# Two transformer layers for four sequences on one core: maxima over bank pairs, one top-k for both tiles, early norm statistics, and new orders on all engines

## The chip, the core and the metric

The kernel runs on one core of a Trainium2 chip. Five engines work side by side: PE (matrix multiply; PEld is its weight load), DVE (vector), ACT (scalar functions), POOL (GpSimd) and SP, which here only issues DMAs. Each works through its own list of instructions in order and waits on semaphores. The metric is the device time of one execution in microseconds (us); lower is better.

## The reference, cut to what matters

The input `x` is 4 sequences (batches) of 256 tokens by 256 features. There are two layers of one form, `x = x + attention(norm(x)) * silu(ffn(norm(x)))`.

```python
xn = _layernorm(x)
s = _L0_attn_ref(xn, ...)              # 32 heads of 8, 8 key/value groups, softmax, no mask
g = _silu(_L0_ffn_ref(xn, ...))        # below
x = x + s * g
xn = _layernorm(x)
s = _L1_attn_ref(xn, ...)              # 16 heads of 16, causal, with slopes by distance
g = _silu(_L1_ffn_ref(xn, ...))        # int8 per token, one 256x256 matmul
x = x + s * g

# _L0_ffn_ref: retrieval among 2048 experts
h = silu(xn @ W_up.T + b_up) @ W_down.T + b_down
sim = (h @ W_q.T) . keys               # 2 halves, 8 heads, 45 keys
scores, idx = lax.top_k(sim, 8)        # per half and head
all_scores = sx[:, None] + sy[None, :] # 64 sums per head
all_indices = ix * 45 + iy
sc, pk = lax.top_k(all_scores, 8)      # 8 experts per head, 64 per token
indices = take_along_axis(all_indices, pk)
z = h . down_embed[indices]
out = (silu(z * softmax(sc))) . up_embed[indices]
```

## The kernel before, in words

The 256 tokens of a batch lie as two tiles of 128 partitions. Each batch goes through the same stages, and a stage `name:b.n` is call `n` for batch `b`. The order in which an engine takes the stages is written out by hand in five tables of words (`PE_PLAN`, `ACT_PLAN`, `DVE_PLAN`, `POOL_PLAN`, `SP_PLAN`); in `PE_PLAN` the digits behind the slash are the PSUM banks that the call takes. There are six such banks (`turn`), one 128x512 f32 tile each; a PE call waits until the earlier user of its bank has been drained (`bank`). Batches overlap: work of batch b+1 stands in the lists between that of batch b.

The stages that the change and the prediction speak of:

- Layer 0's norm (`norm0`, DVE `normalise` L1215): statistics, then an inverse root by three Newton rounds of tiny instructions, then the centring (L1232). `norm1` is the same for layer 1.
- The expert side: `up`, `down` and `sim` on PE give the similarities. DVE finds the top 8 per tile: `topv` (L1255) and `topi` (L1261) on the similarities, `topp` (the 64 sums L1267, their best 8), `topl` (L1284 to L1293: the expert numbers by one-hot products of 128x1024 f32), `topw` (softmax weights). `places` splits the numbers in high and low parts; they go by DRAM (`high`) and come back spread over all partitions (`same`, 1024 KB a load), and `match` (L1323) makes one-hots. PE `pick` (L717) takes the dot products, DVE `pick` (L1339, L1341) selects and sums them, `weigh`/`zs` give the factors.
- Then DVE makes `onehot` (L1362) and `scale` (L1373) for each of eight chunks, PE `spread` (L728) multiplies them, and PE `mix` (L738) multiplies with the table of 16 rows per expert part, one call per tile. PE `table` (L704), ACT `firsts`/`seconds` and POOL `left`/`thirds` (L613, L620) split the first table's products in three bf16 parts.
- Attention of layer 0: `qkv0` on PE, `split0` on DVE (three bf16 parts), `store0`/`stack0` on SP (by DRAM into `stackq`, `stackk`). Then `max0`: PE (L816) computes the scores of one head, DVE (L1397) takes each row's maximum out of PSUM, 32 calls a batch. `nm0` splits the maxima and brings them into the stack by a DMA. `sc0` on PE computes the scores again less the maximum, ACT takes the exponential (L1168), `pv0` (L904) multiplies with the values; `ctx0`, `flip0`, `proj0` and DVE `res0` end the layer.
- Layer 1 has `max1` (L836, L1406), `nm1`, `lift1`, `sc1`, `pv1` and so on, run beside layer 0 of the next batch. After the last batch they run alone.

Layer norms and softmax are exact to f32 parts, so most PE work is f32 or three-part bf16.

## Time and profile before

| what | value |
|---|---|
| time, median of 3 runs | 700.35 us (697.94 to 701.03) |
| profiled execution, first to last instruction | 694.5 us |
| what the median has beyond that span | 5.85 us |
| PE busy | 546.2 us (79%) |
| DVE busy | 499.4 us (72%) |
| ACT busy | 264.1 us (38%) |
| POOL busy | 104.5 us (15%) |
| PE's mean granted clock | 0.860 of full speed |

The page gives the profiled execution by its span alone; the runs are timed apart, and no other time of that execution is listed. No engine is busy throughout: PE and DVE take turns at being the late one, so the shares of the whole say little, and the profile is read stage by stage. A stage is cut here by what DVE and PE do: batch 0's top-k ends at 71.7 us, `nm0` of batches 0 to 3 starts at 138.3, 284.9, 458.3 and 606.3, `max0` of batch 1 starts at 219.0, and `ctx0` of batches 1 to 3 at 345.3, 506.5 and 636.8. Busy times are the engine's own; where one instruction's row overlaps the next, their sum is longer than the stretch.

### The profile page before, as it was taken

To read this page: it belongs to the slowest core of one execution; us is meant where nothing else is said; L and a number is where in the kernel's file an instruction comes from. 1 tells how busy PE (TensorE), PEld (TensorE's weight loads), DVE (VectorE), ACT (ScalarE), POOL (GpSimd) and SP (SyncE) were. 2 spreads that over 40 slices of the span, in tenths; PEclk is the share of its full clock that TensorE was granted. 3 is DMA by queue.
4 is the path that set the end of the run, shared out by engine and by line. 5 is a ranking of instruction groups with operands and counts; after the bars stand their busy time and mean duration, and the time that the engine had idled before them with its cause. 6 is when DMAs were issued, how large, how long until landed. Compare 5 with 4: busy or idle time off the path is not lost.

```text
span 694.5 us, 14791 instructions
## 1 busy us (share of the span) xinstructions
PE 546.2 (79%) x5863; PEld 366.2 (53%) x5863; DVE 499.4 (72%) x1469; ACT 264.1 (38%) x550; POOL 104.5 (15%) x75
## 2 busy tenths in 40 slices
...
GB/s 251 106 128 34 139 123 123 1 4 3 122 50 81 123 124 1 4 2 123 1 54 200 78 47 1 1 3 17 51 164 176 123 2 2 0 19 1 1 1 15
DMA packets 15158, 43.40 MB, mean 62 GB/s; under 512 B 3631, under 2 KB 10927, under 8 KB 11986
## 3 DMA queue, kind: packets, MB, share of 16 engines
...
q10 hardware_dynamic: 396, 0.20, 0.1%
q14 instruction: 22, 0.18, 0.1%
...
## 4 chain that ended last, share of the span: by engine, by line
PE 42%; DVE 42%; issue 10%; ACT 4%; DMA 1%; POOL 1%; SPq 0%; ACTq 0%; DVEq 0%
PE experts L738 8%; DVE nmax L1397 6%; PE outs L904 4%; DVE scaled L1373 4%; PE turn L658 4%; PE turn L867 3%; DVE high_hot L1362 3%; PE turn L883 3%; PE turn L704 2%; DVE z L1341 2%; DVE topi L1261 2%; DVE picks L1339 2%; PE turn L836 2%; DVE nwide L1406 2%; PE turn L728 2%
## 5 line engine op out<-in xcount | busy, mean ns | idle before, releaser
L1168 ACT ACTIVATE probs<-turn 128x512 f32<-128x512 f32 x176 | 97.3, 599 | 54.9 <-PE turn L867 21.4
L1397 DVE TENSOR_REDUCE nmax<-turn 128x2 f32<-128x512 f32 x128 | 87.5, 686 | 41.1 <-PE turn L816 40.1
L613 POOL TENSOR_TENSOR left<-left,dots 128x512 f32<-128x512 f32 x32 | 45.8, 1439 | 344.3 <-ACT dots L1051 344.2
L816 PE MATMUL turn<-stackk,stackq 125*128 125x256 bf16 x256 | 57.6, 325 | 35.3 <-DVE nmax L1397 20.0
L738 PE MATMUL experts<-shared,dots 128*128 128x256 f32 x256 | 59.2, 391 | 0.0
L728 PE MATMUL turn<-scaled,high_hot 128*128 128x32 bf16 x1536 | 44.9, 181 | 16.7 <-issue 7.3
L717 PE MATMUL turn<-dots,shared 128*128 128x32 bf16 x1536 | 44.5, 180 | 16.9 <-DVE shared L1323 8.8
L728 PEld LDWEIGHTS turn<-scaled,high_hot 128*128 128x128 bf16 x1536 | 43.6, 100 | 23.7 <-issue 18.4
L717 PEld LDWEIGHTS turn<-dots,shared 128*128 128x128 bf16 x1536 | 43.3, 99 | 24.1 <-DVE shared L1323 13.2
L1061 ACT ACTIVATE dots<-turn 128x512 f32<-128x512 f32 x32 | 18.8, 595 | 94.5 <-PE turn L728 94.3
L738 PEld LDWEIGHTS experts<-shared,dots 128*128 128x128 f32 x256 | 50.4, 199 | 7.4
L867 PE MATMUL turn<-stackq,stackk 128*128 128x512 bf16 x128 | 46.3, 414 | 6.2 <-issue 4.4
L620 POOL TENSOR_TENSOR dots<-left,dots 128x512 bf16<-128x512 f32 x32 | 48.7, 1538 | 13.3 <-ACT dots L1056 13.3
L816 PEld LDWEIGHTS turn<-stackk,stackq 125*128 125x128 bf16 x256 | 20.4, 105 | 56.8 <-DVE nmax L1397 28.0
L904 PE MATMUL outs<-probs,v 128*32 128x256 f32 x512 | 43.2, 411 | 5.6 <-ACT probs L1168 5.0
L1362 DVE TENSOR_TENSOR high_hot<-turnedh,iotah 128x2048 bf16<-128x2048 bf16 x32 | 41.2, 1292 | 0.7 <-ACT turnedw L1042 0.7
L1323 DVE TENSOR_SCALAR shared<-shared,own 128x4096 bf16<-128x4096 bf16 x16 | 23.1, 1444 | 23.7 <-DMA shared<-scratchh 23.5
L704 PE MATMUL turn<-h2T,down_table 128*128 128x256 f32 x128 | 35.8, 407 | 3.5 <-DVE heads L1442 3.5
L836 PE MATMUL turn<-k,q 32*128 32x128 f32 x384 | 32.9, 318 | 3.7 <-DVE nmaxd L1406 2.0
L1373 DVE TENSOR_TENSOR scaled<-low_hot,factors 128x512 bf16<-128x512 bf16 x96 | 34.7, 415 | 1.4 <-PE turn L728 1.3
L836 PEld LDWEIGHTS turn<-k,q 32*128 32x128 f32 x384 | 27.9, 218 | 13.9 <-issue 13.0
L658 PE MATMUL turn<-xnT,wup 128*128 128x256 f32 x128 | 33.1, 411 | 0.7 <-ACT xnT L985 0.7
...
## 6 DMA issues: line engine op xcount, KB each, us to landing
shared<-scratchh SPq DMA_DIRECT2D x16, 1024.0 KB, 4.9
...
wup<-w_wup SPq DMA_DIRECT2D x1, 1024.0 KB, 5.1
...
```

The lines of the kernel that those rows point to most:

```text
L658: ins = mm(ps[:, a * S:(a + 1) * S], wup[:, c, (2 * j + a) * P:(2 * j + a + 1) * P], xnT[:, c, :], start=(c == 0), stop=(c == DC - 1))
L717: ins = mm(ps[:, k * SPAN:(k + 1) * SPAN], same[:, (QUARTERS * b + q) % 2, t % QUARTER, :], dots[:, t, a, :, :].rearrange("p u l -> p (u l ...
L728: ins = mm(ps[:, k * SPAN:(k + 1) * SPAN], high_hot[:, use % ONE_HOTS, k, :], scaled[:, use % SCALED, a, k, :], start=(a == 0), stop=(a == ...
L738: ins = mm(experts[:, t, :], spreads[:, k, t, :], up_table[:, k, :], start=(k == 0), stop=(k == LO - 1))
L816: ins = mm(ps[:, t * S:(t + 1) * S], stackq[r, m, t * P:(t + 1) * P], stackk[r, m // QUAD, :], start=True, stop=True)
L836: ins = mm(ps[:, j * P:(j + 1) * P], q1[lane(u), j, q], k1[lane(u), k], start=not near, stop=not near or j == QUAD - 1)
L867: mm(bank("sc0", UNITS[0] * b + m)[:, :], stackk[:, u, kc * P:(kc + 1) * P], stackq[:, hd:hd + 2, :], start=True, stop=True).then_inc(fill ...
L904: ins = mm(outs[WIN * strip:WIN * (strip + 1), at], v0[:, kc, lead:lead + WIN], probs[:, nth[0, UNITS[0] * b + AT_ONCE * n + i] % PROBS, S ...
L1168: fn(probs[:, at % PROBS, :], ps[:, :], ACT.Exp).then_inc(exp_done[layer], 1)
L1362: ins = v.tensor_tensor(high_hot[:, use % ONE_HOTS, :, :].rearrange("p t (h r) -> p t h r", r=TWICE), turnedh[:, CHUNK * n:CHUNK * (n + 1) ...
L1373: ins = v.tensor_tensor(scaled[:, use % SCALED, a, :, :].rearrange("p t (l r) -> p t l r", r=TWICE), low_hot[:, at, :].rearrange("p t (l r ...
L1397: v.tensor_reduce(nmax[:, :, m], ps[:, :].rearrange("p (t k) -> p t k", k=S), AX.X, ALU.max, negate=True)\
```

## The change

- `max0` and `max1` work on two heads per call: a call takes two neighbouring banks (`bank_pair`; six banks are three pairs), and one DVE instruction reduces 128x1024 out of both. 128 + 48 reductions become 64 + 24.
- Top-k: `topp`, `topl`, `topw` run once per batch for both tiles. The one-hot products are bf16 (128x2048 each, with pairs of equal elements side by side); the sum over 8 is three halving additions in place of one reduction.
- Norm statistics: a DMA (`early`, 768 KB) brings the x of batches 1 to 3 at the start, and one call (`early:0.0`) takes their statistics and inverse roots at once; `norm0` of those batches is then the centring alone. One instruction fewer in every inverse root.
- DVE's `pick` is split in `pick` (product) and `total` (sum), with two buffers.
- The bias rows of `proj0`/`proj1` are three bf16 parts in one matmul (`partrows`) in place of an f32 one; POOL makes the parts (`bias:0.0`).
- `stack0` is two calls of half the heads (12 DMAs a batch in place of 6), and `max0:b.0` waits for the first half alone. `att_in` weights are issued from ACT's queue.
- All five tables are new. One line each:

```diff
 PE_PLAN = """
-    norm0:0.0/0 up:0.0/1 up:0.1/2 up:0.2/3 fold:0.0/45 up:0.3/0 down:0.0/1 sim:0.0/23 table:0.0/4 sim:0.1/50 qkv0:0.0/12
+    norm0:0.0/0 up:0.0/1 up:0.1/2 qkv0:0.0/34 up:0.2/5 fold:0.0/01 up:0.3/2 down:0.0/3 sim:0.0/45 table:0.0/2 table:0.1/0
...
 DVE_PLAN = """
-    norm0:0.0 hs:0.0 hs:0.1 hs:0.2 hs:0.3 norm0:1.0 topv:0.0 topi:0.0 topp:0.0 split0:0.0 topw:0.0 topl:0.0 topv:0.1 hs:1.0
+    norm0:0.0 early:0.0 hs:0.0 hs:0.1 hs:0.2 hs:0.3 split0:0.0 norm0:1.0 topv:0.0 topi:0.0 topv:0.1 topi:0.1 topp:0.0 hs:1.0
...
+WIDE = {"max0": PAIR, "max1": PAIR}
...
-        turn = [pb(f"turn{n}", [P, 512]) for n in range(BANKS)]
+        pairs = [pb(f"pair{n}", [P, PAIR, 512]) for n in range(BANKS // PAIR)]
+        turn = [pairs[n // PAIR][:, n % PAIR, :] for n in range(BANKS)]
...
-            def stack0(b, _):
+            def stack0(b, n):
...
-                wait_from(sp, filled["sc0"], UNITS[0] * b)
+                wait_from(sp, filled["sc0"], UNITS[0] * (b - 1) + UNITS[0] // LOADED * (n + 1) if b else 0)
...
+            def bias_parts(_, n):
+                pool.wait_ge(late_in, LATE_IN)
...
             def bank(stage, n):
-                earlier = turns.earlier[stage, n]
-                if earlier:
-                    pe.wait_ge(drained[earlier[0]], earlier[1] + 1)
+                for other, k in sorted(turns.earlier[stage, n]):
+                    pe.wait_ge(drained[other], k + 1)
                 return turn[turns.bank[stage, n]]
+
+            def bank_pair(stage, n):
+                bank(stage, n)
+                return pairs[turns.bank[stage, n] // PAIR]
...
             def max0(b, m):
-                if m == 0:
-                    pe.wait_ge(stack_in, STACK_IN * (b + 1))
-                ps, r = bank("max0", H0 * b + m), slice(0, MAX_AT)
-                for t in range(TT):
-                    ins = mm(ps[:, t * S:(t + 1) * S], stackq[r, m, t * P:(t + 1) * P], stackk[r, m // QUAD, :],
-                             start=True, stop=True)
+                if m % (MAXIMA[0] // LOADED) == 0:
+                    pe.wait_ge(stack_in[m // (MAXIMA[0] // LOADED)], STACK_IN * (b + 1))
+                to, r = bank_pair("max0", MAXIMA[0] * b + m), slice(0, MAX_AT)
+                for k in range(PAIR):
+                    h = PAIR * m + k
+                    for t in range(TT):
+                        ins = mm(to[:, k, t * S:(t + 1) * S], stackq[r, h, t * P:(t + 1) * P], stackk[r, h // QUAD, :],
+                                 start=True, stop=True)
...
+            def early_moments(_, n):
+                dve.wait_ge(early_in, 16)
+                moments([early[:, k, :] for k in range((B - 1) * TT)], mv0[:, TT:B * TT, :], rstd0[:, TT:B * TT])
...
-                c.link(v.tensor_copy(full(bestf), bestij))
-                shape = [P, 2 * FH, TOP, TOP]
-                c.link(v.tensor_tensor(full(hot), full(bestf).rearrange("p a h k -> p (a h) k").unsqueeze(3).broadcast_to(shape),
-                                       iota8[:, :].unsqueeze(1).unsqueeze(1).broadcast_to(shape), ALU.is_equal))
...
+                c.link(v.tensor_copy(bestb, bestij.unsqueeze(4).broadcast_to([P, 2, TT * FH, TOP, TWICE])))
...
+                found = hot.rearrange("p g k i -> p (g k) i")
+                for n in (TOP // 2, TOP // 4):
+                    c.link(v.tensor_tensor(found[:, :, 0:n], found[:, :, 0:n], found[:, :, n:2 * n], ALU.add))
+                c.link(v.tensor_tensor(full(picked).rearrange("p a n -> p (a n)"), found[:, :, 0], found[:, :, 1], ALU.add))
...
             def max0(b, m):
...
+                use = MAXIMA[0] * b + m
+                dve.wait_ge(filled["max0"], use + 1)
+                ps = pairs[turns.bank["max0", use] // PAIR]
+                v.tensor_reduce(nmax[:, :, PAIR * m:PAIR * (m + 1)].rearrange("p t h -> p h t"), ps[:, :, :].rearrange("p h (t k) -> p h t k", k=S),
+                                AX.X, ALU.max, negate=True).then_inc(drained["max0"], 1)
```

Where the instructions stand. First DVE in batch 0's top-k. Before, the lookup of the first tile (`topl:0.0`), with the second tile's `topv` behind it (`topf` holds the key numbers, `hot` the one-hots, `picked` the sums):

```order
L1284 TENSOR_SCALAR hot<-bestp 128x64
L1285 TENSOR_SCALAR hot<-bestp 128x64
L1287 CAST bestf<-hot 128x128
L1289 TENSOR_TENSOR hot<-bestf,iota 128x1024
L1291 TENSOR_TENSOR hot<-hot,topf 128x1024
L1292 TENSOR_REDUCE picked<-hot 128x128
L1293 TENSOR_TENSOR place<-picked 128x64
L1255 MAX top<-sims 128x8 x16
```

After, the one lookup of both tiles (`sums` is the memory that the one-hots now lie in):

```order
L1334 TENSOR_SCALAR sums<-bestp 128x128
L1336 CAST picked<-sums 128x512
L1338 TENSOR_TENSOR sums<-picked,iota 128x2048
L1341 TENSOR_TENSOR sums<-sums,topb 128x2048
L1344 TENSOR_TENSOR sums<-sums 128x256x4
L1344 TENSOR_TENSOR sums<-sums 128x256x2
L1345 TENSOR_TENSOR picked<-sums 128x256
L1346 SCALAR_TENSOR_TENSOR bestp<-picked 128x128
L1356 TENSOR_SCALAR sums<-bestp 128x128
```

The lookup stands once, behind both tiles' `topv`, `topi` and `topp`, and goes straight over into `places` (L1356).

Second, DVE at the end of batch 0's maxima. Before, the top-k of batch 1 (`topp:1.0`, `topw:1.0`, `topv:1.1`) stands between the last maxima and `nm0` (L1413):

```order
L1277 MAX_INDEX bestp<-best,hot 128x8 x8
L1279 TENSOR_TENSOR sdiff<-best 128x64
L1397 TENSOR_REDUCE nmax<-turn 128x2
L1312 TENSOR_REDUCE ssum<-sexp 128x8
L1313 RECIPROCAL ssum<-ssum 128x8
L1315 TENSOR_TENSOR wts<-sexp,ssum 128x64
L1397 TENSOR_REDUCE nmax<-turn 128x2
L1255 MAX top<-sims 128x8 x16
L1413 CAST nparts<-nmax 128x2x32
```

After, the same place, from the last step of `zs:0.1` to the second chunk of `onehot` and `scale`:

```order
L1418 TENSOR_TENSOR factors<-zt,factors 128x128
L1461 TENSOR_REDUCE nmax<-pair 128x2x2
L1436 TENSOR_TENSOR scaled<-low_hot,factors 128x512 x3
L1461 TENSOR_REDUCE nmax<-pair 128x2x2 x4
L1478 CAST nparts<-nmax 128x2x32
L1479 TENSOR_TENSOR nrest<-nmax,nparts 128x64
L1480 CAST nparts<-nrest 128x2x32
L1481 TENSOR_TENSOR nparts<-nrest,nparts 128x2x32
L1425 TENSOR_TENSOR high_hot<-turnedh,iotah 128x2048
```

`nm0` follows the maxima at once; the other seven one-hots, seven chunks of `scale` and the whole top-k of batch 1 now stand behind it, beside attention.

Third, PE in batch 3. Before, both calls of `mix` stand among the maxima and layer 1 of batch 2:

```order
L883 MATMUL turn<-q,k 128x512 x2
L816 MATMUL turn<-stackk,stackq 128x256 x2
L738 MATMUL experts<-shared,dots 128x256 x16
L816 MATMUL turn<-stackk,stackq 128x256 x2
L738 MATMUL experts<-shared,dots 128x256 x16
L816 MATMUL turn<-stackk,stackq 128x256 x2
```

After, they stand behind the whole attention of batch 3:

```order
L748 MATMUL pair<-scaled,high_hot 128x32 x48
L949 MATMUL pair<-ident,ctxT 128x128 x8
L758 MATMUL experts<-shared,dots 128x256 x16
L663 MATMUL pair<-ident,heads 128x128 x4
L758 MATMUL experts<-shared,dots 128x256 x16
L971 MATMUL pair<-biases,partrows 128x512
L975 MATMUL pair<-wo,headsT 128x256 x4
```

`mix:3.0` and `mix:3.1` moved from the maxima to between `ctx0:3.0` (L949) and `proj0:3.0` (L971).

## Rows read from the trace of the kernel before

**Rows 1.** Windows: length; busy us (count) PE, PEld, DVE, ACT, POOL; PE clock; DMA
```profile
0.00:28.50 28.50, 19.00 (x93) 15.18 (x94) 10.08 (x41) 10.91 (x27) 10.75 (x11) 1.00 0.52 167
28.50:71.70 43.20, 22.60 (x104) 17.73 (x102) 42.44 (x181) 24.30 (x53) 23.57 (x16) 0.74 0.32 98
71.70:138.30 66.60, 36.10 (x653) 25.85 (x653) 64.90 (x205) 6.34 (x15) 0.00 (x0) 0.68 0.27 101
138.30:219.00 80.70, 66.55 (x549) 45.83 (x549) 48.72 (x124) 46.82 (x97) 25.36 (x16) 0.92 0.17 56
219.00:284.90 65.90, 50.77 (x827) 38.27 (x827) 63.92 (x178) 9.29 (x20) 0.52 (x1) 0.77 0.18 65
284.90:506.50 221.60, 201.84 (x2008) 127.85 (x2004) 163.62 (x506) 111.02 (x222) 44.34 (x32) 0.90 0.15 51
506.50:606.30 99.80, 80.75 (x1115) 60.57 (x1114) 75.22 (x153) 16.99 (x35) 0.00 (x0) 0.85 0.22 69
606.30:636.80 30.50, 27.44 (x225) 9.03 (x223) 3.42 (x9) 22.62 (x43) 0.00 (x0) 1.00 0.04 11
636.80:694.50 57.70, 41.09 (x300) 25.91 (x300) 27.12 (x81) 15.84 (x39) 0.00 (x0) 0.91 0.02 5
```

**Rows 2.** DVE in order of time, batch 0's lookup: start us, us
```profile
44.37 2.20 DVE L1291 TENSOR_TENSOR hot<-hot,topf 128x1024 f32<-128x1024 f32 x1
46.61 1.22 DVE L1292 TENSOR_REDUCE picked<-hot 128x128 f32<-128x1024 f32 x1
```

**Rows 3.** DVE in order of time: batch 2's norm0, then batch 1's first tile
```profile
74.36 0.74 DVE L1219 BATCH_NORM_STATS2 stats<-xnext 128x6 f32<-128x256 f32 x2
...
77.79 0.74 DVE L1232 TENSOR_SCALAR th_up<-xnext,mv,rstd 128x256 f32<-128x256 f32 x2
...
130.99 0.68 DVE L1267 TENSOR_TENSOR hot<-top 128x512 f32<-128x512 f32 x1
...
134.62 0.69 DVE L1397 TENSOR_REDUCE nmax<-turn 128x2 f32<-128x512 f32 x1
...
139.14 0.19 DVE L1284 TENSOR_SCALAR hot<-bestp 128x64 uint32<-128x64 uint32 x1
...
140.98 1.23 DVE L1291 TENSOR_TENSOR hot<-hot,topf 128x1024 f32<-128x1024 f32 x1
...
143.49 0.23 DVE L1293 TENSOR_TENSOR place<-picked 128x64 uint32<-128x64 f32 x1
```

**Rows 4.** The chain that ended last, batch 0's first tile: start us, us
```profile
28.57 1.73 DVE top L1255 x16
30.32 2.91 DVE topi L1261 x17
```

**Rows 5.** Lines kept apart by form: busy us, mean ns, idle before, releasers
```profile
L1397 DVE TENSOR_REDUCE nmax<-turn 128x2 f32<-128x512 f32 x128 | 87.5, 686 | 41.1 <-PE turn L816 40.1
L738 PE MATMUL experts<-shared,dots 128*128 128x256 f32 x256 | 59.2, 391 | 0.0
L816 PE MATMUL turn<-stackk,stackq 125*128 125x256 bf16 x256 | 57.6, 325 | 35.3 <-DVE nmax L1397 20.0 <-DMA stackk<-scratchk 14.2 <-DVE picks L1339 0.6
L728 PE MATMUL turn<-scaled,high_hot 128*128 128x32 bf16 x1536 | 44.9, 181 | 16.7 <-issue 7.3 <-DVE nmax L1397 4.0 <-DVE scaled L1373 2.4
L1362 DVE TENSOR_TENSOR high_hot<-turnedh,iotah 128x2048 bf16<-128x2048 bf16 x32 | 41.2, 1292 | 0.7 <-ACT turnedw L1042 0.7
L704 PE MATMUL turn<-h2T,down_table 128*128 128x256 f32 x128 | 35.8, 407 | 3.5 <-DVE heads L1442 3.5
L1373 DVE TENSOR_TENSOR scaled<-low_hot,factors 128x512 bf16<-128x512 bf16 x96 | 34.7, 415 | 1.4 <-PE turn L728 1.3
L836 PE MATMUL turn<-k,q 32*128 32x128 f32 x384 | 32.9, 318 | 3.7 <-DVE nmaxd L1406 2.0 <-issue 1.0 <-ACT q L1114 0.7
```

**Rows 6.** DMA issues: count, KB each, median us from issue to landing
```profile
shared<-scratchh SPq DMA_DIRECT2D x16, 1024.0 KB, 4.9
```

**Rows 7.** PE in order of time, batch 1's first maximum: wait in brackets
```profile
219.04 0.61 PE L816 MATMUL turn<-stackk,stackq 125*128 125x256 bf16 x4 [2.75 <-DMA stackk<-scratchk]
```

More of the change, by code:

```diff
@@ L89 @@
-    pv0:0.7 sc0:0.18/5 sc0:0.19/4 sc0:0.20/3 pv0:0.8 sc0:0.21/1 pv0:0.9 sc0:0.22/0 spread:0.6/2 sc0:0.23/5 pv0:0.10 sc0:0.24/4
-    spread:0.7/3 sc0:0.25/1 pv0:0.11 sc0:0.26/0 mix:0.0 sc0:0.27/2 mix:0.1 sc0:0.28/5 pv0:0.12 sc0:0.29/4 pv0:0.13 sc0:0.30/3
-    table:1.0/1 sc0:0.31/0 pv0:0.14 table:1.1/2 turnw:1.0/5 pv0:0.15 qkv0:1.0/43 ctx0:0.0/10 table:1.2/2 norm0:2.0/5 table:1.3/1
-    up:2.0/3 up:2.1/4 flip0:0.0/2 table:1.4/5 up:2.2/1 table:1.5/0 proj0:0.0/3 up:2.3/4 table:1.6/5 table:1.7/2 down:2.0/1
@@ L192 @@
-    onehot:2.7 max0:2.14 scale:2.7 max0:2.15 lift1:1.0 max0:2.16 max0:2.17 max0:2.18 max0:2.19 max0:2.20 max0:2.21 max0:2.22
-    max0:2.23 max1:1.4 max0:2.24 max1:1.5 max0:2.25 max0:2.26 max1:1.6 max0:2.27 max1:1.7 max1:1.8 max0:2.28 max1:1.9 max0:2.29
-    max0:2.30 max1:1.10 max0:2.31 max1:1.11 nm0:2.0 nm1:1.0 topv:3.0 topi:3.0 lift1:1.1 topp:3.0 over1:1.0 topl:3.0 topw:3.0
-    fin1:0.0 topv:3.1 round1:1.0 topi:3.1 out1:1.0 over1:1.1 topp:3.1 topl:3.1 topw:3.1 places:3.0 fin1:1.0 lowhot:3.0
@@ new lines @@
+    max0:0.9 weigh:0.1 max0:0.10 zs:0.1 max0:0.11 scale:0.0 max0:0.12 max0:0.13 max0:0.14 max0:0.15 nm0:0.0 onehot:0.1 scale:0.1
+    scale:0.2 onehot:0.2 scale:0.3 onehot:0.3 scale:0.4 onehot:0.4 scale:0.5 onehot:0.5 scale:0.6 onehot:0.6 scale:0.7
+    onehot:0.7 topv:1.0 topi:1.0 topv:1.1 topi:1.1 topp:1.0 topw:1.0 topl:1.0 places:1.0 norm0:2.0 match:1.0 over0:0.0
+    split0:1.0 over0:0.1 onehot:1.0 lowhot:1.0 res0:0.0 match:1.1 res0:0.1 norm1:0.0 max0:1.0 hs:2.0 max0:1.1 round1:0.0
+    max0:1.2 pick:1.0 hs:2.1 pick:1.1 total:1.0 hs:2.2 max0:1.3 total:1.1 hs:2.3 pick:1.2 match:1.2 pick:1.3 total:1.2 max0:1.4
@@ new lines @@
+    pick:1.4 total:1.3 max0:1.5 weigh:1.0 total:1.4 zs:1.0 match:1.3 max0:1.6 pick:1.5 max0:1.7 pick:1.6 total:1.5 max0:1.8
+    total:1.6 pick:1.7 total:1.7 weigh:1.1 max0:1.9 zs:1.1 max0:1.10 max0:1.11 max0:1.12 max0:1.13 max0:1.14 max0:1.15 nm0:1.0
+    scale:1.0 onehot:1.1 scale:1.1 onehot:1.2 scale:1.2 onehot:1.3 scale:1.3 onehot:1.4 scale:1.4 onehot:1.5 scale:1.5 scale:1.6
+    onehot:1.6 scale:1.7 onehot:1.7 out1:0.0 topv:2.0 max1:0.0 topi:2.0 topv:2.1 topi:2.1 topp:2.0 max1:0.1 topl:2.0 max1:0.2
```

553 lines of the change are left out of this document (297 added, 256 removed).

## The prediction

> **What bounds the kernel now.** I read the windows view first, stage by stage, because the shares of the whole name no engine. In [rows 1] compare length with busy time. From 28.5 to 138.3 us DVE is busy 42.44 of 43.2 and 64.90 of 66.6, while PE is busy half of the time: batch 0's top-k, lookup and maxima run at DVE's pace. From 138.3 to 219 neither is full (PE 66.55, DVE 48.72 of 80.7). From 219 to 284.9 DVE is the bound again (63.92 of 65.9). From 284.9 to 506.5 it is PE (201.84 of 221.6, 91%). From 506.5 to 606.3 PE has 80.75 and DVE 75.22 of 99.8; then DVE is nearly idle (3.42 of 30.5). The last 57.7 us are a chain in which PE is idle for 16.6. I call these stretches A (to 28.5), B (to 138.3), C, D, E, H, I and J, and make the sum over them, against the profiled span of 694.5. The median of the runs, 700.35, lies 5.85 above that span; I add the same to the forecast's span.
>
> **A and B, 138.3 us, DVE's list.** The clearest items are those that leave it.
>
> - Lookup. One tile's `topl` runs from 139.14 to 143.49 plus 0.23, 4.58 us [rows 3]; two are 9.2. In batch 0 it is dearer, since its product took 2.20 in place of 1.23, while the reduction stayed at 1.22 [rows 2, 3]. After, both tiles share one. Two bf16 products of 128x2048: the nearest row is the one-hot of that size and type, 1.29 [rows 5]; at the f32 pace of 1.23 per 1024 they would be 2.45 each. Halving additions of 1024, 512 and 256 outputs by the same pace are 0.65, 0.32 and 0.23 (at the f32 pace 1.23, 0.61, 0.23). The cast to 512 is at most 0.62, three small steps are 0.23 each. That is 5.1 to 8.3; I take 5.4, as the one-hot's row has the same shape and type: 3.8 saved.
> - Batch 1's `topv` twice (1.73 each), a `topi` (2.91) [rows 4] and one `topp` (130.99 to 134.62, 3.63 [rows 3]) move behind `nm0`: 10.0.
> - Five `scale` chunks (1.08 each) and three `onehot`s (1.29) [rows 5] move there too: 5.4 + 3.9.
> - Norm statistics of batch 2: one `norm0` is 78.53 - 74.36 = 4.17, of which the centring's 0.74 stays [rows 3]: 3.4.
> - Maxima: the two-bank reduction of 128x1024 has no row. Its ends are two of L1397's, 1.37 [rows 5], and the 1.22 of a reduction of that size from SBUF [rows 2]; I take 1.22. 16 x 0.15 = 2.4.
> - `split0` moves ahead of the top-k, into DVE's 18.4 idle us of A [rows 1]. By size (three steps of 128x768 at 1.23 per 1024) it is 2.8.
> - DVE's steps beside POOL: each two-input step there pays about 0.97 (2.20 against 1.23 [rows 2, 3]). Fewer of them now lie beside POOL's 23.57 busy us of B; between 0 and 8, I take 3, as three steps.
>
> Together 34.7. POOL's contention needs a closer look, because the change replaces a reduction, which the rows show unslowed, by three two-input additions. At 0.97 each, all three would give back 2.9 of the lookup's 3.8 in batch 0, and nothing later, where POOL is quiet. The Trainium skill ("GPSIMD Engine Reference", section "Specifications") says that GpSimd's SBUF interfaces are shared with VectorE and that the contention is with VectorE instructions that read two SBUF inputs or run in a two-port mode. By it the reduction is exempt and the three additions are not, as the rows have it, and the time would be up to 2.9 worse, 656; by the nearest product row alone it stays 653.
>
> Added to the path: `qkv0` now stands on PE ahead of `up:0.2`, and early statistics ahead of `hs:0.0` on DVE. Everything of the expert side is queued behind both. The bounds are 0 and PE's whole idle time in A, 9.5 [rows 1]; I take the middle, 5. The early load of 768 KB is less than the 1024 KB that land in 4.9 us [rows 6], so its wait, at most 3.7, lies within this; its six statistics and one root lie in DVE's idle 18.4. The two `same` loads of batch 0 now come when DVE has less to do beside them: one of 4.9 could be bare, I take 2. The bias parts lie in POOL's idle 17.7 us of A and cost nothing; without that cover they would delay only `proj0`, far later. A and B: 138.3 - 34.7 + 7 = 110.6.
>
> **C and D, 146.6 us.** What DVE was rid of before `nm0` arrives here (19.3), yet C has 32.0 us of idle DVE [rows 1]. In D DVE loses six `scale` (6.5), four `onehot` (5.2), eight single reductions of layer 1 (5.5, by L1397's mean), one `topv` and `topi` (4.6), one norm (4.2) and the pairs' 2.4: 63.9 falls to 35.5, and some hidden-layer steps without a row add 2 to 4. So DVE stops being D's bound. Next late is PE: 117.3 in C and D, plus three `spread` (4.2) less one `table` (1.1) in C, less five `spread` (7.0) and five `max1` (6.9) in D: 106.4. The calls of `up` and `down` that move from C to D cancel. PE's share is 82% in C and 91% in E; I take between, 86.5%, since a pair gives DVE and PE longer strides: 123. DVE would then be 100 of 123 (112.6 + 19.3, less 28.4 in D and 3.8 of a lookup). The halves of `stack0` can remove the wait of 2.75 at batch 1's first maximum [rows 7], part of 14.2 for that load in all [rows 5]. SP issues six more DMAs a batch for it, ahead of whatever it issues next; I count neither apart.
>
> **E, 221.6.** The five `spread` (7.0) and five `max1` (6.9) come here, three `table` (3.4) go: PE 212.3 at 91% gives 233. Here the change costs 11.5, because PE has no room.
>
> **H and I, 130.3.** Both `mix` of batch 3 leave (16 matmuls of 7.4 each way, 14.8 [rows 5]), two `table` come (2.2): PE 95.6. DVE's remaining `onehot` and `scale` of batch 3 move into I, where DVE was busy 3.42 of 30.5. At the old 83% it is 115, at 91% 105; I take 113.
>
> **J, 57.7.** `mix` (14.8) now stands between `ctx0:3.0` and `proj0:3.0`, with PE in order behind it: this is the last chain, so it is not free. It can be hidden from nothing to all of 14.8 in PE's idle 16.6; the idle time is spread over waits for DVE and ACT, so I take a quarter, 4.5, with the cheaper bias matmul and root in it: 68.
>
> **Sum.** 110.6 + 123 + 233 + 113 + 68 = 647.6, and 653 with the 5.85: 47 us less. Most is DVE's work taken off the path in B and D (51); E and J give back 22.
>
> **Rivals.**
>
> 1. Only the stretch before `nm0:0` gains in full; after it the engines hand the wait to each other and half of the gain in C, D, H and I is lost: C and D 135, H and I 122, J 70, sum 670.6, 676 us. For it: PE idles 35.3 us at L816, of it 20.0 for DVE's maxima, and DVE 40.1 for L816 [rows 5], so neither is late alone.
> 2. The new orders pack PE closer, 93% from C to I (414.3 / 0.93 = 445): with 110.6 and 66 for J 622, 628 us. For it: L816's 35.3 idle us, and PE's 29.3 in C and D. Against it: DVE would then be over 80% in every stretch.
>    The Trainium skill ("Perfetto Trace Analysis", section "Identifying the Most-Contended Engine") holds matmul busy time to be a bad measure of headroom and the weight loads' share a good one. In E PEld is 127.85 of 221.6, 58%, beside PE's 91%. By that rule E has room and could fall rather than rise. No row here shows how much of PE's time the loads would let go, so the rule bears on rival 2's chance alone.
> 3. Slower: bank pairs collide. There are three pairs only, and the single-bank calls of `spread`, `sc0` and `table` take banks out of the same pairs. PE, in order, waits for both banks, DVE waits until both are filled, and each of the 88 pair calls exposes the filling of two heads, 57.6 / 64 = 0.90 [rows 5]. If all did, 79 us would be added: 732. From 52 calls on the kernel is not faster; at three quarters it is 713. For it: DVE idles 40.1 us for L816 already. Against it: the tables place other stages' calls between neighbouring maxima.
> 4. The edits don't do what they say: bf16 products at the f32 pace (up to 3.2 per batch, felt in B alone), early statistics bare, lookups off the path, and `mix` fully bare: with rival 1 this ends within 0.5% of before.
>
> **How the numbers follow.** Forecast 0.47 (637 to 668, its terms' bounds: A 0 to 9.5, lookup 3.2, POOL -5 to +3, J -10 to +4.5, PE's share in C and D 84 to 91%); rival 1 0.23; rival 2 0.18; rival 3 0.07; rival 4 0.05. 0.5% (696.8 to 703.9) is about what a measurement of this kernel can tell from no change. Rival 4 gives 0.04 within it and the rest just below. Faster: 0.47 + 0.23 + 0.18 + 0.01 = 0.89; same 0.04; slower 0.07. The range of 622 to 690 leaves out the slow rivals and the best ends of rival 2.
>
> **What would show it.** In the profile after, `nm0:0` should start near 110; the pair reduction should take about 1.2, and the lookup 5.4 once per batch; DVE should be below 90% between batch 1's first maximum and `nm0:1`; PE should stay above 90% from there to `ctx0:2`; J should be near 68 with both `mix` in it. I am wrong if the pair reduction takes over 1.37, if PE's waits for `nmax` exceed the 20.0 of before [rows 5], if `nm0:0` starts after 120, or if J is over 75.

## The result, and the profile after

The changed kernel takes 612.42 us (median of 4 runs, 611.09 to 613.8), the kernel before 700.05 beside it: ratio 0.8752, 95% interval 0.8732 to 0.8773. The forecast was 653, its range 622 to 690: right in sign, too small by 41 us, and outside the range.

The windows view of the changed kernel, cut at the same marks as [rows 1] (columns as there; C and D, and A and B, in one):

```profile
0.00:112.86 112.86, 71.47 (x705) 56.06 (x705) 87.09 (x269) 37.37 (x85) 43.06 (x36) 0.82 0.41 143
112.86:230.90 118.04, 97.14 (x1175) 72.95 (x1183) 103.54 (x289) 52.92 (x114) 23.34 (x16) 0.91 0.22 77
230.90:443.67 212.77, 198.77 (x2316) 135.83 (x2330) 181.29 (x530) 107.77 (x220) 40.30 (x26) 0.97 0.16 55
443.67:510.44 66.77, 52.32 (x700) 35.96 (x699) 62.60 (x99) 19.54 (x41) 11.09 (x7) 0.90 0.28 98
510.44:545.62 35.18, 32.41 (x573) 18.54 (x580) 19.57 (x41) 22.85 (x44) 0.00 (x0) 0.90 0.02 4
545.62:611.90 66.28, 52.97 (x367) 36.60 (x363) 27.08 (x74) 17.15 (x42) 0.00 (x0) 0.90 0.03 9
```

Against the terms of the sum:

| stretch | before | forecast | after | miss |
|---|---|---|---|---|
| A and B | 138.3 | 110.6 | 112.9 | +2.3 |
| C and D | 146.6 | 123 | 118.0 | -5.0 |
| E | 221.6 | 233 | 212.8 | -20.2 |
| H and I | 130.3 | 113 | 102.0 | -11.0 |
| J | 57.7 | 68 | 66.3 | -1.7 |
| median beyond the span | 5.85 | 5.85 | 0.5 | -5.3 |

The last line is no work: the profiled execution after was timed at 613.8 for its span of 611.9, 1.9 more, and the rest of the 5.85 was that the profiled execution of before was a quick one. In E look at the third row beside [rows 1]: PE has 308 more recorded matmuls than before (2316 against 2008), yet is busy 3 us less, at a clock of 0.97 in place of 0.90, and its idle time is 14.0 in place of 19.8. DVE is busy 181.3 of 212.8, where it was 163.6 of 221.6. Some matmul records are missing: L889 has 97 matmuls and 128 weight loads in the whole trace, and 15 of the missing ones, of about 0.37 us, belong to E. The run one_head below takes as long and has all its records; there PE is busy 200.5 of E's 211.5.

Two of the costliest lines of the profile after, to be read beside [rows 5] (busy us, mean ns, idle before):

```profile
L1461 DVE TENSOR_REDUCE nmax<-pair 128x4 f32<-128x1024 f32 x64 | 77.0, 1219 | 7.8 <-PE pair L838 7.6
...
L838 PE MATMUL pair<-stackk,stackq 125*128 125x256 bf16 x256 | 42.2, 297 | 12.9 <-DVE nmax L1461 6.1
```

The pair reduction takes 1.219, as taken from [rows 2]. PE waits 6.1 for `nmax` (20.0 before), DVE 7.6 for the maxima (40.1 before): bank pairs do not collide as rival 3 had it.

The one lookup, in batch 2 (DVE in order of time: start us, us):

```profile
275.99 2.35 DVE L1338 TENSOR_TENSOR sums<-picked,iota 128x2048 bf16<-128x2048 bf16 x1
278.37 2.20 DVE L1341 TENSOR_TENSOR sums<-sums,topb 128x2048 bf16<-128x2048 bf16 x1
280.60 2.35 DVE L1344 TENSOR_TENSOR sums<-sums 128x1024 bf16<-128x1024 bf16 x2
282.99 1.57 DVE L1345 TENSOR_TENSOR picked<-sums 128x256 f32<-128x256 bf16 x1
```

With its small steps it takes 10.7 us here, and 8.3 to 8.8 in the other batches, where 5.4 was taken out of 5.1 to 8.3. Two of the lookups lie in E.

### The profile page after: what moved, and what is told of

The parts are those of the page before. It is cut to its first block and busy times, and to the rows that moved or that the text cites. A ratio compares the mean times of both kernels' runs of the same rounds, so it can differ in the third digit from the quotient of the medians.

```text
span 611.9 us, 14570 instructions
## 1 busy us (share of the span) xinstructions
PE 505.1 (83%) x5823; PEld 355.9 (58%) x5854; DVE 481.2 (79%) x1298; ACT 257.6 (42%) x546; POOL 117.8 (19%) x84
## 5 line engine op out<-in xcount | busy, mean ns | idle before, releaser
L1194 ACT ACTIVATE probs<-pair 128x512 f32<-128x512 f32 x176 | 98.0, 607 | 78.5 <-PE pair L905 45.4
L1461 DVE TENSOR_REDUCE nmax<-pair 128x4 f32<-128x1024 f32 x64 | 77.0, 1219 | 7.8 <-PE pair L838 7.6
L737 PE MATMUL pair<-dots,shared 128*128 128x32 bf16 x1536 | 43.6, 181 | 21.0 <-issue 9.5
L737 PEld LDWEIGHTS pair<-dots,shared 128*128 128x128 bf16 x1536 | 42.4, 99 | 25.8 <-issue 17.6
L624 POOL TENSOR_TENSOR dots<-left,dots 128x512 bf16<-128x512 f32 x32 | 49.9, 1570 | 35.9 <-ACT dots L1081 35.9
L838 PE MATMUL pair<-stackk,stackq 125*128 125x256 bf16 x256 | 42.2, 297 | 12.9 <-DVE nmax L1461 6.1
L748 PEld LDWEIGHTS pair<-scaled,high_hot 128*128 128x128 bf16 x1536 | 42.5, 96 | 8.2 <-issue 4.8
L1436 DVE TENSOR_TENSOR scaled<-low_hot,factors 128x512 bf16<-128x512 bf16 x96 | 34.7, 418 | 13.5 <-PE pair L748 13.4
L926 PE MATMUL outs<-probs,v 128*32 128x256 f32 x512 | 42.2, 406 | 2.7 <-issue 1.7
L748 PE MATMUL pair<-scaled,high_hot 128*128 128x32 bf16 x1536 | 43.7, 177 | 0.8 <-issue 0.6
L724 PE MATMUL pair<-h2T,down_table 128*128 128x256 f32 x128 | 35.9, 410 | 5.4 <-DVE nwide L1471 4.6
L889 PE MATMUL pair<-stackq,stackk 128*128 128x512 bf16 x97 | 34.4, 398 | 5.2 <-DMA stackq<-nmaxT 3.0
L678 PE MATMUL pair<-xnT,wup 128*128 128x256 f32 x128 | 34.6, 420 | 2.9 <-ACT xnT L1008 2.8
L889 PEld LDWEIGHTS pair<-stackq,stackk 128*128 128x128 bf16 x128 | 11.0, 98 | 33.9 <-issue 14.4
```

The source lines that it names most:

```text
L624: nc.gpsimd.tensor_tensor(dots[:, :, 2, :, PER_BANK * n:PER_BANK * (n + 1)], left[:, use % RESTS, :, :, :], at, ALU.subtract).then_inc(thi ...
L678: ins = mm(ps[:, a * S:(a + 1) * S], wup[:, c, (2 * j + a) * P:(2 * j + a + 1) * P], xnT[:, c, :], start=(c == 0), stop=(c == DC - 1))
L737: ins = mm(ps[:, k * SPAN:(k + 1) * SPAN], same[:, (QUARTERS * b + q) % 2, t % QUARTER, :], dots[:, t, a, :, :].rearrange("p u l -> p (u l ...
L748: ins = mm(ps[:, k * SPAN:(k + 1) * SPAN], high_hot[:, use % ONE_HOTS, k, :], scaled[:, use % SCALED, a, k, :], start=(a == 0), stop=(a == ...
L838: ins = mm(to[:, k, t * S:(t + 1) * S], stackq[r, h, t * P:(t + 1) * P], stackk[r, h // QUAD, :], start=True, stop=True)
L889: mm(bank("sc0", UNITS[0] * b + m)[:, :], stackk[:, u, kc * P:(kc + 1) * P], stackq[:, hd:hd + 2, :], start=True, stop=True).then_inc(fill ...
```

## The experiments

All times are medians. The stretches are those of the table; `after` is the changed kernel. E's three parts are cut at `ctx0:1` and `nm0:2`. Each stretch is read from one profiled execution. Where after, pe_more and dve_more run the same work, A and B read 112.9, 110.4 and 113.5 us, C and D 118.0, 119.0 and 117.3, and H 66.8, 67.4 and 66.8, while E's middle part reads 94.2 in all three; smaller differences say nothing.

| run | us | ratio to before, 95% | A, B | C, D | E (its parts) | H | I | J |
|---|---|---|---|---|---|---|---|---|
| after | 612.4 | 0.873 to 0.877 | 112.9 | 118.0 | 212.8 (66.5, 94.2, 52.2) | 66.8 | 35.2 | 66.3 |
| new_orders | 674.6 | 0.961 to 0.970 | 118.0 | 130.1 | 248.7 (83.4, 101.1, 64.2) | 73.6 | 35.4 | 66.7 |
| new_orders2 | 657.2 | 0.936 to 0.949 | 118.0 | 126.7 | 234.1 (74.5, 101.4, 58.2) | 70.7 | 36.4 | 67.7 |
| old_orders | 689.5 | 0.982 to 0.993 | 126.8 | 152.2 | 225.9 (66.8, 109.3, 49.9) | 93.0 | 30.1 | 59.3 |
| split_drain | 615.1 | 0.874 to 0.883 | 113.8 | 118.7 | 212.6 | 67.5 | 36.0 | 66.4 |
| norm_late | 622.2 | 0.885 to 0.894 | 117.4 | 120.0 | 215.6 (65.0, 98.2, 52.3) | 66.4 | 35.9 | 65.7 |
| one_head | 613.0 | 0.874 to 0.881 | 110.7 | 118.5 | 211.5 (65.2, 94.0, 52.3) | 67.3 | 35.9 | 66.3 |
| tile_topk | 624.7 | 0.891 to 0.896 | 119.3 | 120.5 | 216.1 (63.0, 95.3, 57.8) | 67.4 | 35.0 | 65.8 |
| tile_topk_late | 637.8 | 0.909 to 0.917 | 119.4 | 122.5 | 226.7 (74.4, 94.2, 58.1) | 67.4 | 34.8 | 65.7 |
| small_back | 628.5 | 0.897 to 0.905 | 112.9 | 120.9 | 214.0 (64.7, 96.1, 53.2) | 75.7 | 34.7 | 66.2 |
| spread_back | 626.9 | 0.891 to 0.899 | 111.9 | 125.6 | 217.8 (66.8, 97.2, 53.8) | 68.2 | 36.0 | 66.5 |
| spread3_back | 635.1 | 0.905 to 0.910 | 113.5 | 119.0 | 217.4 | 90.1 | 30.0 | 66.5 |
| mix_back | 651.5 | 0.927 to 0.935 | 113.3 | 120.0 | 216.5 | 90.1 | 44.2 | 68.5 |
| pe_more | 639.3 | 0.912 to 0.917 | 110.4 | 119.0 | 239.3 (79.0, 94.2, 66.1) | 67.4 | 34.7 | 66.3 |
| dve_more | 627.9 | 0.897 to 0.901 | 113.5 | 117.3 | 226.2 (72.9, 94.2, 59.2) | 66.8 | 35.1 | 66.3 |
| one_reduce | 603.8 | 0.863 to 0.870 | 109.7 | 116.9 | 206.2 (63.3, 94.2, 48.7) | 66.8 | 34.6 | 66.3 |
| reduce_one_head | 605.0 | 0.863 to 0.867 | 110.4 | 118.9 | 203.7 (60.9, 94.0, 48.9) | 67.6 | 35.9 | 66.3 |

### Orders and edits apart

**new_orders**, the kernel before with all five tables of after; a pair's call becomes two, on the pair's two banks:

```diff
-    max0:0.0/2 max0:0.1/4 max0:0.2/3 max0:0.3/0 table:0.7/5 max0:0.4/2
+    max0:0.0/2 max0:0.1/3 max0:0.2/0 max0:0.3/1 up:1.1/5 turnw:0.0/4 max0:0.4/2 max0:0.5/3 table:0.7/5
```

> The kernel before with the new five orders alone: one-head maxima (both heads of a pair one behind the other), top-k per tile, the statistics in each norm, f32 bias rows, the stack in one piece. Theory A (the stretch from batch 1's split maxima to batch 2's ctx, 284.9 to 506.5 before, fell to 212.8 because the new orders feed PE without gaps): that stretch is 212 to 218 here too, its granted clock at least 0.95, and the whole takes 655 to 668 us. Rival B (it fell because the edits make the work cheaper): the stretch stays at 222 to 235 with the clock near 0.90, and the whole takes 680 to 695 us.

E grew to 248.7, against both theories. My own translation was part of it: the weights stood ahead of the lookup, so DVE waited 11.1 us there for ACT's exponential. **new_orders2** puts that right:

```diff
-    topp:2.0 max1:0.2 max1:0.3 topw:2.0 topl:2.0 topv:2.1 topi:2.1 topp:2.1 topw:2.1 topl:2.1
+    topp:2.0 max1:0.2 max1:0.3 topl:2.0 topv:2.1 topi:2.1 topw:2.0 topp:2.1 topl:2.1 topw:2.1
```

> As new_orders (the kernel before under the new orders), with one thing put right in its order: in each tile's top-k the lookup now stands between the pairs' sums and the softmax weights, so DVE need not stand still for ACT's exponential (11.1 us of such waits in new_orders' stretch from nm0 of batch 1 to ctx0 of batch 2, beside one PE wait of 21.1 for a bank that DVE drains behind the top-k). Theory E (that stretch was long, 248.7, because of this chain of top-k, ACT and the bank): it falls to 220 to 228, the whole to 650 to 660 us. Rival F (it is long because the work of before is dearer under these orders): 240 to 250, the whole 668 to 675 us.

E is 234.1, between the two theories, and the whole as theory E had it: the orders alone give 42 us of the 88, and leave E as long as the forecast had it (233).

**old_orders**, the edits under the tables of before:

```diff
-    topv:0.1 hs:1.0 topi:0.1 hs:1.1 topp:0.1 hs:1.2 topw:0.1 max0:0.0 topl:0.1 max0:0.1
+    topv:0.1 hs:1.0 topi:0.1 hs:1.1 topp:0.0 hs:1.2 topw:0.0 topl:0.0 max0:0.0
```

> The changed kernel's edits under the orders of before, in which two neighbouring maxima are merged at the place of one of them and the PSUM banks are dealt out anew for the pairs. Theory A (the orders do most): 670 to 685 us, the stretch from nm0 of batch 1 to ctx0 of batch 2 at 218 to 225. Rival B (the edits do most): 630 to 650 us, the stretch at 208 to 214.

689.5, above both theories: the edits alone give 11 us. A and B are 11.5 shorter and H 6.8, C and D are 5.6 longer, and E does not gain (225.9). The two together give more than their sum (88 against 53). Both translations are by hand, so the split is rough.

### One edit of the changed kernel undone

**split_drain** and **one_head**: DVE's part of the pairs (shown for layer 0; layer 1 is cut the same way), then the whole pair.

```diff
-v.tensor_reduce(nmax[:, :, PAIR * m:PAIR * (m + 1)] ..., ps[:, :, :] ...)
+for k in range(PAIR):
+    ins = v.tensor_reduce(nmax[:, :, PAIR * m + k], ps[:, k, :] ...)
```

> The changed kernel, but each pair of banks is reduced by two instructions of 128x512 in place of one of 128x1024; PE still fills two heads per call. The one took 1.219 us, two take 1.37: 0.15 more in each of 88 calls, 13 us of DVE in all. Theory A (DVE still sets the pace where the maxima stand): 8 to 13 us longer, 620 to 626 us. Rival C (what pairs bring is the fewer handovers between PE and DVE, not DVE's time): 0 to 3 us longer, 612 to 616 us.

```diff
-WIDE = {"max0": PAIR, "max1": PAIR}
+WIDE = {}
-    max0:0.0/2 max0:0.1/0
+    max0:0.0/2 max0:0.1/3 max0:0.2/0 max0:0.3/1
```

> The changed kernel with one-head maxima: each call of a pair is two calls of one bank each, in the same places and banks, and DVE reduces one bank per instruction. Theory A (a pair is worth what two small reductions cost more than a large one, 2.7 us in split_drain, and a little of PE's filling): 613 to 618 us. Rival C (the fewer handovers of the pairs carry the gain): 625 to 640 us. Rival G (a pair holds two banks longer than it saves): 605 to 611 us.

615.1 and 613.0: the pairs are worth 0 to 3 us, less than the 13 us of DVE that they save.

**norm_late**, without the early statistics:

```diff
-                if b == 0:
-                    moments([xnext[:, t, :] for t in range(TT)], mv0[:, 0:TT, :], rstd0[:, 0:TT])
+                moments([xnext[:, t, :] for t in range(TT)], mv0[:, TT * b:TT * (b + 1), :], rstd0[:, TT * b:TT * (b + 1)])
```

> The changed kernel without the early statistics: each norm0 takes its own, as before, and the 768 KB load is gone. Theory A: 3.4 us of DVE come back in batches 1 to 3; in the first 113 us, where DVE sets the pace, that costs 3.4, later up to 3.4 each: 616 to 622 us. Rival D (the early load and its statistics delay the first stretch by as much as they save): 608 to 613 us.

622.2, the far end of theory A: 4.5 in A and B, 2.0 in C and D (hardly more than unchanged work differs by), and 4.0 in E's middle part, where `norm0:3` stands.

**tile_topk** and **tile_topk_late**: the top-k per tile, in two orders (DVE, batch 2).

```diff
-    topv:2.0 max1:0.0 topi:2.0 topv:2.1 topi:2.1 topp:2.0 max1:0.1 topl:2.0
+    topv:2.0 max1:0.0 topi:2.0 topp:2.0 topl:2.0 topv:2.1 topi:2.1 topp:2.1 max1:0.1 topl:2.1
```

> The changed kernel with its top-k taken per tile: the pairs' sums, the lookup (bf16 still, 128x1024 per tile) and the weights are two instructions' worth each, tile 0's lookup standing between the searches of both tiles, both weights where the one stood. Theory J (the stretch from nm0:1 to ctx0:2 lives by the one top-k of both tiles; it was 234.1 under the new orders with the code of before and is 212.8 here): 227 to 232 there, 630 to 640 us in all. Rival K (it lives by the other edits): 213 to 217 there, 614 to 620 us.

216.1 in E, as rival K had it, and 624.7 in all, between the two theories: what is dearer per tile is 12 us, half of it in A and B. The second order is the one that the one-tile buffers of before need:

```diff
-    topl:2.0 topv:2.1 topi:2.1 topp:2.1 max1:0.1 topl:2.1 max1:0.2 max1:0.3 topw:2.0 topw:2.1
+    max1:0.1 topl:2.0 topv:2.1 topi:2.1 topw:2.0 topp:2.1 topl:2.1 topw:2.1 max1:0.2 max1:0.3
```

> As tile_topk, but in the order that the code of before needs (its buffers hold one tile: tile 0's weights, and with them ACT's exponential, must come ahead of tile 1's sums), so tile 1's whole top-k stands where the lookup stood, behind a reduction of layer 1 whose bank PE waits for. If that order is what the stretch from nm0:1 to ctx0:2 pays for under new_orders2 (234.1 against 216.1 in tile_topk): 224 to 232 there and 633 to 645 us. If not, and the rest of the code of before is: 214 to 219 there, 622 to 628 us.

E is 226.7, as the first reading had it, and its first and last part are those of new_orders2 within 0.1. Waits in E (us in total, times, longest), first of new_orders2, then of tile_topk_late, then of after:

```profile
PE turn L867 <- DVE nwide L1406: 12.8, 1, 12.8
PE outs L904 <- ACT probs L1168: 4.6, 2, 4.4
```

```profile
PE pair L890 <- DVE nwide L1473: 13.0, 1, 13.0
PE outs L927 <- ACT ctxT L1208: 9.3, 1, 9.3
ACT sdiff L1102 <- DVE sdiff L1325: 17.3, 2, 9.1
```

```profile
PE pair L724 <- DVE nwide L1471: 4.6, 1, 4.6
PE pair L715 <- DVE gate L1566: 3.5, 1, 3.5
```

The same wait of 13 us stands in both, in E's first part: PE needs the bank of a layer-1 maximum, which DVE drains behind tile 1's top-k. The changed kernel waits 4.6 there. The last part is longer by another wait. ACT, in order, stands for 9.1 us behind tile 1's exponential, whose input DVE makes late, and PE stands for 9.3 behind ACT. tile_topk has this second wait too (8.8 us, and a last part of 57.8), new_orders2 a part of it (4.4); the changed kernel takes one exponential for both tiles and has none there.

**small_back**: each sum behind its product, and one wait for the whole stack.

```diff
-                if m % (MAXIMA[0] // LOADED) == 0:
-                    pe.wait_ge(stack_in[m // (MAXIMA[0] // LOADED)], STACK_IN * (b + 1))
+                if m == 0:
+                    for half in stack_in:
+                        pe.wait_ge(half, STACK_IN * (b + 1))
-    pick:1.0 hs:2.1 pick:1.1 total:1.0
+    pick:1.0 total:1.0 hs:2.1 pick:1.1 total:1.1
```

> The changed kernel with each sum over the picks straight behind its product again, and the maxima waiting for both halves of the stack, as before. Theory K (such small waits carry the stretches of maxima): 618 to 626 us. Theory J: 612 to 616 us.

628.5, a little over theory K's range, most of it in H (75.7, 8.9 more). The two edits were put back together, but the trace tells them apart in part. Batch 3's first maximum waits for the second half of the stack, which SP issues from 470.9 to 475.1 us:

```profile
479.83 1.01 PE L839 MATMUL pair<-stackk,stackq 125*128 125x256 bf16 x4 [5.75 <-issue]
```

The wait for the whole stack is thus 5.75 of the 8.9; the other 3.1 stay open.

### Where moved work stands

**spread_back**, batch 1's chunks ahead of `nm0:1` again:

```diff
-    max0:1.11 max0:1.12 max0:1.13 max0:1.14 max0:1.15 nm0:1.0 scale:1.0 onehot:1.1 scale:1.1
+    scale:1.0 max0:1.11 onehot:1.1 scale:1.1 max0:1.12 onehot:1.2 scale:1.2 max0:1.13 onehot:1.3 scale:1.3 max0:1.14
```

> The changed kernel with spread, onehot and scale of batch 1's first five chunks moved back ahead of nm0:1, as before the change. By the prediction's step (PE has no room behind nm0:1, each chunk costs there): the stretch behind nm0:1 falls by 7 us to about 206, the one ahead of it grows by DVE's 10.6: 615 to 617 us. Rival H (the stretch behind nm0:1 has room, its length is set by waits that stay): it keeps 211 to 213 and the one ahead grows by 10: 621 to 624 us.

C and D grew by 7.6. E did not fall by 7 but grew by 5.0, so that the whole is above both forecasts. The growth of E is not the chunks' doing. This edit and the next two also deal out PE's banks anew, from the first stage on: of the 447 calls that take banks, 336 to 357 take others. The next two runs move nothing into E or out of it, and their E grew as well, by 4.6 and 3.7 us, with the same last part of 53.8. Beside mix_back's E (216.5), taking five chunks out of E gave nothing. The first part (up to `ctx0:1`) of spread_back, then of mix_back:

```profile
237.47:304.29 66.82, 58.64 (x556) 35.53 (x555) 45.37 (x189) 31.64 (x63) 12.50 (x9) 0.87 0.08 28
```

```profile
233.30:299.06 65.76, 59.96 (x749) 40.00 (x747) 55.13 (x208) 33.94 (x67) 12.49 (x9) 0.95 0.08 30
```

With 193 matmuls fewer PE is busy only 1.3 us less, at a clock of 0.87 against 0.95, and the part is no shorter.

**mix_back** and **spread3_back**, batch 3's chunks among the maxima again, with and without `mix`:

```diff
-    max0:3.13 max0:3.14 max0:3.15 over1:2.0 nm0:3.0 scale:3.0 onehot:3.1 scale:3.1
+    scale:3.3 onehot:3.4 max0:3.13 scale:3.4 onehot:3.5 max0:3.14 scale:3.5 onehot:3.6 max0:3.15 scale:3.6 onehot:3.7
-    ctx0:3.0/42 mix:3.0 flip0:3.0/3 mix:3.1 proj0:3.0/5
+    pv0:3.1 mix:3.0 sc0:3.7/2 sc0:3.8/3 sc0:3.9/1 pv0:3.2 sc0:3.10/0 pv0:3.3 mix:3.1
```

> The changed kernel with batch 3's onehot, scale, spread and mix moved back to the maxima and the start of attention. By the prediction's steps: the stretch from ctx0:2 to nm0:3 grows by DVE's 16 us (62.6 of 66.7 are busy already), attention falls by 4, the tail by 10: 612 to 616 us. Rival I (mix is hidden in the tail's idle PE, so the tail gains nothing back): the tail stays within 3 us of 66.3 and the whole takes 622 to 628 us.

> As mix_back, but both mix of batch 3 stay behind its attention: only onehot, scale and spread of batch 3 go back among the maxima. If mix_back's 40 us came from DVE's 16 us ahead of nm0:3 and what hangs on them: the stretch ctx0:2 to nm0:3 is again about 90, attention 30 to 33 in place of 44, the tail 66: 632 to 640 us. If they came from where mix stands (its place lets PE's clock fall in the tail): 615 to 625 us.

H is 90.1 in both, 23 more than after, and I falls by 5; spread3_back is as its first reading had it, mix_back far above both of its forecasts. DVE is busy 15.2 us more in H (77.8), and waits 8.0 for PE's `spread` to free the one-hots, which it does not in after:

```profile
DVE high_hot L1425 <- PE pair L748: 8.0, 3, 5.8
```

No run tells whether the new banks have a part in that wait. Moving `mix` as well costs 14.2 more in I and gives nothing back in J. Two rows of mix_back's tail (8 us each) show why:

```profile
608.00:616.00 8.00, 7.20 (x74) 5.37 (x72) 6.29 (x12) 1.52 (x6) 0.00 (x0) 0.83 0.01 2
616.00:624.00 8.00, 8.00 (x30) 3.15 (x30) 1.80 (x3) 1.47 (x3) 0.00 (x0) 0.50 0.00 0
```

From 616 to 640 PE is busy all the time at the lower clock, 1.2 GHz; over the whole tail the clock is 0.69, where after has 0.90.

### Which engine sets E

**pe_more** and **dve_more** add work to one engine, in E alone (`mix` of batches 1 and 2 twice over; the one-hot product of batches 2 and 3 six times):

```diff
-                for k in range(LO):
+                for k in [*range(LO)] * (2 if b in (1, 2) else 1):
```

> The changed kernel with each mix call of batches 1 and 2 done twice over (64 more matmuls of 128x256, 28.4 us of PE, all in the stretch from nm0:1 to ctx0:2). If PE has no room there, as the prediction had it: the stretch grows by 27 to 29, 640 us in all. If part falls into PE's waits and the lists of the other engines set the rest: 15 to 24 longer, 628 to 636 us.

```diff
-                c.link(v.tensor_tensor(hot..., bestb..., iota8..., ALU.is_equal))
+                for _ in range(6 if b in (2, 3) else 1):
+                    c.link(v.tensor_tensor(hot..., bestb..., iota8..., ALU.is_equal))
```

> The changed kernel with the lookup's one-hot product of batches 2 and 3 done six times in place of once: ten more DVE instructions of 128x2048, 1.23 to 2.35 us each, 12 to 23 us, in the same stretch, where PE is the busier engine. If PE sets its length (the prediction's step): 0 to 5 longer, 612 to 617 us. If DVE's list sets it as much (one_reduce took 6.6 from it with some 4 us of DVE): 12 to 23 longer, 624 to 636 us.

E of pe_more, then of dve_more:

```profile
229.39:468.69 239.30, 225.35 (x2442) 159.12 (x2456) 181.62 (x530) 107.65 (x220) 39.95 (x26) 0.98 0.14 49
```

```profile
230.78:456.97 226.19, 200.12 (x2316) 136.23 (x2330) 193.61 (x540) 108.10 (x220) 44.52 (x26) 0.94 0.15 52
```

26.6 us more of PE (225.35 against 198.77) lengthen E by 26.5; 12.3 us more of DVE (193.61 against 181.29) lengthen it by 13.4. Both lists are on the path, one behind the other, in the two attention parts; the middle part keeps 94.2 in both. The waits of PE that after shows above grow in dve_more by what DVE was given, 6.2 and 5.9:

```profile
PE pair L724 <- DVE nwide L1472: 10.8, 1, 10.8
PE pair L715 <- DVE gate L1567: 9.4, 1, 9.4
```

L724 is a `table` whose bank DVE drains behind the top-k; L715 turns the top-k's own numbers and weights. In one_reduce, next, the two waits are 1.9 and 1.3.

**one_reduce** and **reduce_one_head**: the lookup's three additions become one reduction again, then with one-head maxima too (the edit of one_head).

```diff
-                for n in (TOP // 2, TOP // 4):
-                    c.link(v.tensor_tensor(found[:, :, 0:n], found[:, :, 0:n], found[:, :, n:2 * n], ALU.add))
-                c.link(v.tensor_tensor(full(picked)..., found[:, :, 0], found[:, :, 1], ALU.add))
+                c.link(v.tensor_reduce(full(picked)..., found, AX.X, ALU.add))
```

> The changed kernel with one reduction of 128x2048 in place of the three halving additions of the lookup, which took 3.9 to 5.0 us a batch instead of the 1.2 in the prediction's sum. Theory L (two-input additions pay beside POOL, a reduction does not): the reduction takes 2.44 (two of 1.22) everywhere, the lookup falls from 8.3 to 10.7 us by 1 to 2.5, and the whole is 609 to 611 us. Rival M (the lookup is hidden): 611.5 to 613.5 us.

The step of the lookup above that stands for its three additions, in one_reduce:

```profile
276.40 2.29 DVE L1343 TENSOR_REDUCE picked<-sums 128x256 f32<-128x2048 bf16 x1
```

2.29 in place of 3.92. In all E's DVE is busy 5.6 us less, and E is 6.6 shorter: 603.8 us, better than both kernels and than both theories.

> one_reduce with one-head maxima as well. one_head alone made no difference: 602 to 605 us. If the finer handover lets DVE's saved time be used: 597 to 601 us.

605.0: no further gain.

## Why the prediction was wrong

**The step, 36 of the 41 us.** From C to I the sum takes for each stretch PE's busy time of before, adds and takes away the matmuls that move, and divides by a share. The shares came out near. The step that failed is the busy time, which the prediction carried over from before; in E that is "PE 212.3 at 91% gives 233. Here the change costs 11.5, because PE has no room."

| stretch | PE busy: forecast, after | share: forecast, after |
|---|---|---|
| C and D | 106.4, 97.1 | 86%, 82% |
| E | 212.3, 198.8 | 91%, 93% |
| H and I | 95.6, 84.7 | 85%, 83% |

Together PE is busy 33.7 us less than forecast, and the three stretches are 36.2 shorter. Missing records are the lesser part of that: one_head, which has them all and takes 613.0, has 100.4, 200.5 and 86.0, together 27.4 less than forecast. A matmul's time was taken from a trace in which PE often stood still, and it did not stay: the clock rose from 0.85 to 0.91 in C and D, from 0.90 to 0.97 in E and from 0.88 to 0.90 in H and I, and the 256 matmuls of the layer-0 maxima took 42.2 us in place of 57.6 [rows 5]. No run changes the clock alone, so how much of the 27 to 34 us is clock, and how much is matmuls that no longer start one by one behind waits, stays open.

**E, 20 of the 41 us: the waits.** PE has no room for more work (pe_more), and DVE's work in the lookups costs its full length (dve_more). The prediction credited every saving of DVE to A to D, and DVE's 163.6 of 221.6 in E [rows 1] was read as cover. It is none: PE, in order, stands first behind a bank that DVE drains behind the top-k, then behind the top-k's numbers. The forecast of 233 beside new_orders2's 234.1 is partly luck: PE is busy 208.5 there, not 212.3, and 12.8 and 4.6 us of its waits are not in the forecast. Of the 21.3 us between new_orders2 and the changed kernel, the one-tile top-k with the order that it forces is 13.9 (tile_topk_late: 8.0 in the first part, by the bank, and 5.9 in the last, by ACT; 3.3 of E is left without that order, tile_topk). The middle part's 7.2 are the statistics of `norm0:3` (4.0, norm_late), the sums and the halves of the stack (1.9, small_back), and 1.3 that no run gives; the whole of E grew by only 2.8 and 1.2 in those two runs, since their first parts came out shorter.

**H and I, 11 us.** The term went by PE's busy time and a share of 83 to 91%. In H the late engine is DVE: 62.60 of 66.77 after, 77.81 of 90.09 in spread3_back. Taking DVE's work out of H is worth up to 23 us there (15.2 of DVE's own, 8.0 of its waits for PE) and costs 5 in I. The direction was right, the engine was not.

**C and D, 5 us.** DVE's work came down to 103.5 of 118.0 (100 of 123 forecast). But DVE did not stop being D's bound: between batch 1's first maximum and `nm0:1`, where it was to be below 90%, it is busy 45.65 of 48.50, 94%. The total is near although the term went by PE, which is partly luck.

**A and B, J.** Right within 2.3 and 1.7, the first with errors that cancel: the lookup takes 8.3 in place of 5.4, the pairs (2.4) are worth little, and the statistics (3.4) 4.5. The bias parts, put into POOL's idle time of A at no cost, stand at 52.8 to 60.0 us, beside that lookup.

**The weighed rule on POOL's interface** held, and was priced too low. In after's lookups the additions take 3.0 to 4.9 us a batch; in one_reduce the reduction takes 2.29 in every batch, and the kernel is 8.6 us faster, where at most 2.9 was given. By the Trainium skill ("GPSIMD Engine Reference", section "Specifications") the two-input additions contend and the reduction does not; the traces agree. In batch 3 the first addition ends before POOL's next product and takes 0.69 us; the two that follow, half and a quarter of its size, lie beside POOL and take 1.69 and 1.64. "Nothing later, where POOL is quiet" was misread: POOL is busy beside all four lookups, and in [rows 1] 25.36 us in C and 44.34 in E.

**Rivals.** Rival 2 (PE packs closer, 628) came nearest, but not by its mechanism: from C to I PE's share is 88%, not 93%, and its busy time 380.6 us, not 414.3. The Trainium skill's rule that the weight loads' share shows headroom ("Perfetto Trace Analysis", section "Identifying the Most-Contended Engine") is borne out by half in E: E fell, with more matmuls in it, but PEld is at 64% there (135.83 of 212.77), and work added to PE still cost 26.5 of 26.6. Rival 3 did not occur. The range was too narrow at its lower end, since rival 2's chance was given to one mechanism and no term let E fall.
